# Writing out an inner loop of TensorE in the forward transform of a Fourier tower

## The chip, the cores and the metric

One core of one Trainium2 chip runs the whole program. The metric is device time in microseconds (us) from launch to end, the median of several executions of the same program. All arithmetic is float32.

## The reference, cut to what matters

The input is 64 images of 64x64 pixels with 3 channels. A tower of four Fourier layers works on 64 channels. Each layer adds a spectral convolution (a 2-D Fourier transform, a product with complex 64x64 matrices for 32x16 low modes, and the inverse) to a 64x64 pointwise map, normalizes over batch and pixels, and applies GELU. Attention and two mixtures of experts follow; the change does not touch them.

```python
for l in range(LAYERS):                                   # 4
    sc = _spectral_conv(h, w1r[l] + 1j * w1i[l], w2r[l] + 1j * w2i[l])
    pw = jnp.einsum('bihw,oi->bohw', h, pw_w[l]) + pw_b[l][None, :, None, None]
    y = sc + pw
    ...
    h = jax.nn.gelu(y, approximate=False)
```

## The kernel before, in words

Two images make a pair (128 partitions = 2 x 64 channels), four pairs (Q = 4) make a group, and there are NG = 8 groups, so 32 pairs. Each layer runs in phases, with a meeting of all engines between them (`phase_end`): **forward** (the transform of the layer's input to its low modes), **mix** (the complex product) and **inverse** (back to pixels, pointwise map, statistics). The first layer's forward phase has its own code. Layers 1 to 3 share one body: every engine has an outer hardware loop `Fori(1, L)` over them, so the forward phase that concerns us runs three times, from the same instructions.

In the forward phase every pair goes through five steps:

- SyncE loads the pair's 2 MB from `y_dram` into one of four buffers `hf` (L767 to L792). A buffer is free again when VectorE has turned the pair that was in it.
- ScalarE applies normalization and GELU in four pieces (`scalar_forward`, L843).
- VectorE transposes those four pieces (`px_turn`, L848).
- TensorE does the transform along the width (`w_dft`, L796, matmuls at L803), VectorE transposes the result out of PSUM in two pieces (`w_turn`, L853), and TensorE does the transform along the height (`h_dft`, L809, matmuls at L820).
- VectorE transposes that out of PSUM in two pieces (`h_turn`, L862), and once a group is complete SyncE stores it to `spec_in`.

TensorE's order is written by hand: `w_dft(n)`, then `h_dft(n-1)`, pair after pair. Before `w_dft(n)` it waits for the four transposed pieces of pair n and for the width result of the pair before to be out of PSUM (L797, L798); before `h_dft` it waits for `w_turn` and for the height result of the pair before to be out (L811, L812). VectorE's order, also fixed, is three `px_turn` of pair p, two `w_turn` of pair p-1, the `h_turn` of pair p-2, and the fourth `px_turn` of pair p (L865 to L875). The buffers `t1` and `hT` alternate by the parity of the pair and the PSUM banks are the same for all pairs. The other engines' streams of the forward phase are already written out over all 32 pairs; only TensorE has a hardware loop inside the phase: it does group 0 by itself and then `Fori(1, NG)` over groups 1 to 7, with the four pairs of a group written out in its body. Semaphore thresholds in it are computed from the loop's register and from the layer's.

[...]

Of the kernel before, what the change touches and what calls it, by code (L numbers as in the profile page):

```python
# [102 lines left out]
def build(nc, d, B, out):  # L103

    NP, NG = B // 2, B // GI
# [3 lines left out]
    with ExitStack() as ctx:  # L109
# [684 lines left out]
        def tensor_forward(pe, lf):  # L794
            def w_dft(n, q):

                pe.wait_ge(px_turned, n * 4 + (4 * Q + 4))  # L797
                pe.wait_ge(wdft_turned, n * 2 + 2)  # L798
                pe.sem_inc(waited[pe.engine], 1)
                for s in range(2):  # L800
                    for g in range(4):
                        for c in range(4):
                            mm = pe.matmul(bank[g][QUAD[c], :], fwq[QUAD[g], s * 32:(s + 1) * 32],  # L803
                                           hT[q % 2][QUAD[g], s, :, c * CQ:(c + 1) * CQ],
                                           start=(s == 0), stop=(s == 1), tile_position=(32 * g, 32 * c))
                        if s == 1:
                            mm.then_inc(wdft_done, 1)

            def h_dft(n, q):  # L809

                pe.wait_ge(wdft_turned, n * 2 + 4)  # L811
                pe.wait_ge(hdft_turned, n * 2 + 2)  # L812
                pe.sem_inc(waited[pe.engine], 1)
                for k in range(4):
                    hh, ri = k // 2, k % 2
                    for j in range(4):
                        ro, v = j // 2, j % 2
                        col = (k * 2 + ro) * K1
                        for c in range(4):
                            mm = pe.matmul(bank[4 + c][QUAD[j], 0:256], ghq[QUAD[c], col:col + K1],  # L820
                                           t1[q % 2][QUAD[c], v:4:2, hh, :, ri * M2:(ri + 1) * M2],
                                           start=(k == 0), stop=(k == 3), tile_position=(32 * c, 32 * j))
                mm.then_inc(hdft_done, 1)

            def group(F, first):
                for q in range(Q):
                    n = F * Q + q
                    w_dft(n, q)
                    if q > 0 or not first:
                        h_dft(n - 1, (q - 1) % Q)  # L830

            group(lf * NG, True)
            with pe.Fori(1, NG) as g:
                group(lf * NG + g, False)
            h_dft(lf * NP + (NP - 1), Q - 1)

        def scalar_forward(act, lf):
# [1124 lines left out]
        @block.tensor  # L1962
        def _(pe):
            tensor_spectrum0(pe)
            phase_end(pe, 1)
            tensor_mix(pe, 0, True)
            phase_end(pe, 2)
            tensor_inverse(pe, 0, True)
            phase_end(pe, 3)
            with pe.Fori(1, L) as l:  # L1970
                tensor_forward(pe, l - 1)
                phase_end(pe, l * 3 + 1)
                tensor_mix(pe, l, False)
                phase_end(pe, l * 3 + 2)
                tensor_inverse(pe, l, False)
                phase_end(pe, l * 3 + 3)
            tensor_head(pe)
            phase_end(pe, TOWER + 1)
            tail_tensor(pe)
# [112 lines left out]
```

## Time and profile before

| | before |
|---|---|
| median of 3 runs | 4440.83 us (4436.05 to 4450.31) |
| the profiled execution | 4442.78 us, span 4441.0 us |
| granted TensorE clock, mean | 0.868 |
| busy: PE, PEld, DVE, ACT | 74%, 47%, 54%, 47% |
| mean DMA rate | 252 GB/s |

The span is from the first to the last instruction; the execution's own time is 1.8 us longer. PE is TensorE's matrix multiply, PEld its weight load, which runs beside it; DVE is VectorE, ACT ScalarE, SP SyncE. [...]

### The profile page before, as it was taken

The page shows a single profiled execution, that of the slowest core. Times are in us where ns is not written, and L with a number is a line of the kernel's source. Part 1 is how long each engine was busy: PE and PEld are TensorE (multiplying, and loading weights), DVE is VectorE, ACT ScalarE, POOL GpSimd, SP SyncE. Part 2 cuts the span into 40 slices and gives each one's busy share as a digit, 9 for nine tenths or more (in the row PEclk, how much of TensorE's full clock was granted, in tenths as well). Part 3 has the DMA queues.
Part 4 walks back from the last instruction along what each step waited for, and adds up shares of the span by engine and source line. Part 5 has one row for each costly group of instructions (what it writes and reads, how often), then busy time and mean ns, then how long its engine had stood idle before and what let it go on. Part 6 is the DMA issues. An engine that isn't in the chain of part 4 may idle for free. (4 is left out here: it accounts for less than half of the span.)

```text
span 4441.0 us, 122046 instructions
## 1 busy us (share of the span) xinstructions
PE 3288.5 (74%) x54724; PEld 2081.7 (47%) x54724; DVE 2394.9 (54%) x3232; ACT 2086.9 (47%) x1724; POOL 28.9 (1%) x48
## 2 busy tenths in 40 slices
PE   6878866666888565596886556768877998559777
PEld 4756644455555343473554334745542222543432
DVE  3466668753666587544665777346651000554556
ACT  2133354421666644214665543236667998222321
POOL 0000000000000000000000000000000000100000
PEclk8989988888999888898998778989998999669688
DMA  8978887678999867598999676889996542003053
GB/s 305 351 192 241 238 265 271 256 288 336 345 391 380 295 249 264 228 327 330 381 377 333 248 264 249 321 294 399 391 340 231 190 173 99 10 10 68 1 97 67
DMA packets 181646, 1120.67 MB, mean 252 GB/s; under 512 B 25497, under 2 KB 31841, under 8 KB 107262
## 3 DMA queue, kind: packets, MB, share of 16 engines
q1 hardware_dynamic: 140924, 843.27, 52.7%
q10 hardware_dynamic: 39234, 269.45, 17.5%
q8 instruction: 379, 6.21, 0.5%
q0 software_dynamic: 1024, 1.05, 0.1%
q14 instruction: 85, 0.70, 0.0%
HBM read 708.56 MB, written 405.14 MB: 251 GB/s over the span
## 5 line engine op out<-in xcount | busy, mean ns | idle before, releaser
L602 PEld LDWEIGHTS bank<-fb,arena 64*64 64x64 f32 x16384 | 671.9, 199 | 512.9 <-issue 498.8
L602 PE MATMUL bank<-fb,arena 64*64 64x128 f32 x16384 | 677.9, 293 | 236.8 <-ACT arena L659 183.2
L659 ACT ACTIVATE arena<-bank,pwb 128x1024 f32<-128x1024 f32 x512 | 558.7, 1111 | 472.5 <-PE bank L593 337.0
L703 DVE BATCH_NORM_STATS2 stats<-arena 128x6 f32<-128x512 f32 x1024 | 627.8, 676 | 176.4 <-ACT arena L659 175.9
L843 ACT ACTIVATE arena<-arena,shift,scale 128x1024 f32<-128x1024 f32 x384 | 443.5, 1229 | 438.4 <-DMA arena<-y_dram 437.9
L593 PE MATMUL bank<-arena,wst 64*64 64x512 f32 x4096 | 629.9, 633 | 11.0 <-issue 10.9
L695 DVE STREAM_TRANSPOSE arena<-bank 128x512 f32<-128x512 f32 x512 | 321.1, 685 | 501.5 <-PE bank L579 501.5
L803 PE MATMUL bank<-arena,fwq 32*32 32x512 f32 x6144 | 322.6, 824 | 362.4 <-DVE arena L848 319.3
L651 ACT ACTIVATE arena<-arena,shift,scale 128x2048 f32<-128x2048 f32 x192 | 401.4, 2092 | 353.4 <-issue 206.2
L444 PE MATMUL bank<-arena 64*64 64x128 f32 x8192 | 455.4, 393 | 108.0 <-ACT arena L459 89.0
L444 PEld LDWEIGHTS bank<-arena 64*64 64x64 f32 x8192 | 395.0, 153 | 168.1 <-issue 118.8
L848 DVE STREAM_TRANSPOSE arena<-arena 128x1024 f32<-128x1024 f32 x384 | 440.1, 1203 | 16.2 <-ACT arena L843 16.2
L820 PE MATMUL bank<-arena,ghq 32*32 32x256 f32 x12288 | 366.0, 429 | 49.6 <-issue 45.1
L579 PE MATMUL bank<-arena,ga 64*64 64x512 f32 x2048 | 307.7, 619 | 127.8 <-DMA arena<-spec_out 108.5
L820 PEld LDWEIGHTS bank<-arena,ghq 32*32 32x32 f32 x12288 | 281.7, 111 | 140.5 <-issue 109.1
L803 PEld LDWEIGHTS bank<-arena,fwq 32*32 32x32 f32 x6144 | 101.0, 117 | 496.6 <-issue 486.0
L459 ACT ACTIVATE arena<-arena 64x4096 f32<-64x4096 f32 x32 | 115.9, 3621 | 448.2 <-DMA arena<-spec_in 448.2
L480 DVE STREAM_TRANSPOSE arena<-bank 128x512 f32<-128x512 f32 x256 | 159.5, 683 | 253.3 <-PE bank L444 134.8
L919 PE MATMUL bank<-arena,fc 64*128 64x512 f32 x1024 | 265.3, 626 | 17.9 <-ACT arena L947 16.5
L954 ACT ACTIVATE arena<-bank,fc1b 128x1024 f32<-128x1024 f32 x256 | 267.8, 1122 | 14.3 <-PE bank L919 14.3
L853 DVE STREAM_TRANSPOSE arena<-bank 128x1024 f32<-128x1024 f32 x192 | 227.2, 1221 | 84.9 <-PE bank L803 84.4
L579 PEld LDWEIGHTS bank<-arena,ga 64*64 64x64 f32 x2048 | 115.4, 138 | 249.9 <-issue 236.5
(195 smaller groups left out, 2364.4 us busy)
## 6 DMA issues: line engine op xcount, KB each, us to landing
arena<-y_dram SPq DMA_DIRECT2D x224, 2048.0 KB, 10.2
y_dram<-arena ACTq DMA_DIRECT2D x256, 1024.0 KB, 13.2
arena<-in_w_modes SPq DMA_DIRECT2D x32, 2048.0 KB, 17.2
arena<-spec_in SPq DMA_DIRECT2D x32, 2048.0 KB, 14.7
spec_out<-arena SPq DMA_DIRECT2D x128, 512.0 KB, 15.6
arena<-spec_out SPq DMA_DIRECT2D x112, 512.0 KB, 16.9
spec_in<-arena SPq DMA_DIRECT2D x24, 2048.0 KB, 13.6
spec_in<-arena SPq DMA_DIRECT2D x4, 4096.0 KB, 12.0
```

The lines of the kernel that those rows point to most:

```text
L444: mm = pe.matmul(bank[4 * v + q][ROW[half], k * 2 * B:(k + 1) * 2 * B], w_sb[u][ROW[row], mode, :], s_sb[u][ROW[row], :, :, mode], start=( ...
L579: mm = pe.matmul(bank[2 * v + r][CHAN[par], :], ga[k_p, r * S:(r + 1) * S], grp[p // Q % 2][k_p, :, par * Q + q, :], start=True, stop=True ...
L593: mm = pe.matmul(bank[4 + T % 2 * 2 + i][CHAN[v], :], wst[CHAN[i], :], hin[p % 3][CHAN[i], px:px + BK], start=False, stop=True, tile_posit ...
L602: mm = pe.matmul(hpx(bank[4 + T % 2 * 2 + i][CHAN[v], :])[:, :, j * S:(j + 1) * S], a2[p % 2][CHAN[i], v, :, 4 * T + j], hpx(fb2[CHAN[i], :]),
L651: act.activation(x, x, ACT.Gelu, bias=shift[:], scale=scale[:]).then_inc(h_ready, 1)
L659: act.activation(hpx(yout[u])[:, :, T * BK:(T + 1) * BK], banks[:, 4 + T % 2 * 2:6 + T % 2 * 2, :], ACT.Identity, bias=pwb[:]).then_inc(y_ ...
L695: dve.transpose(a2[p % 2][:, :, v * HB + c0:v * HB + c0 + 16, :].rearrange("p v c r -> p c v r"), banks[:, 2 * v:2 * v + 2, :].rearrange(" ...
L703: dve.bn_stats(stats[:, p * 48 + 6 * t:p * 48 + 6 * t + 6], hpx(yout[p % 2])[:, i, T * BK:(T + 1) * BK]).then_inc(y_seen, 1)
L803: mm = pe.matmul(bank[g][QUAD[c], :], fwq[QUAD[g], s * 32:(s + 1) * 32], hT[q % 2][QUAD[g], s, :, c * CQ:(c + 1) * CQ], start=(s == 0), st ...
L820: mm = pe.matmul(bank[4 + c][QUAD[j], 0:256], ghq[QUAD[c], col:col + K1], t1[q % 2][QUAD[c], v:4:2, hh, :, ri * M2:(ri + 1) * M2], start=( ...
L843: act.activation(x, x, ACT.Gelu, bias=shift[:], scale=scale[:]).then_inc(f_ready, 1)
L848: dve.transpose(hT[p % 2][:, :, 16 * v:16 * v + 16, :].rearrange("p s h c -> p h s c"), hf[p % Q][:, v * 2 * BK:(v + 1) * 2 * BK].rearrang ...
```

## The change

TensorE's groups of the forward phase are all written out. Group 0 still begins without the `h_dft` of a pair before it. Nothing that TensorE computes and no order changes, the semaphore thresholds are the same numbers (they still hold the layer's register), and no other engine's stream is touched. The outer loop over layers stays.

```diff
-            group(lf * NG, True)
-            with pe.Fori(1, NG) as g:
-                group(lf * NG + g, False)
+            for g in range(NG):
+                group(lf * NG + g, g == 0)
             h_dft(lf * NP + (NP - 1), Q - 1)
```

## Rows read from the trace of the kernel before

**Rows 1.** Busy time by stage: the three forward phases, one mix, one inverse
```profile
core 0: us, PE busy (x) PEld busy (x) DVE busy (x) ACT busy (x) POOL busy (x), PEclk, DMA share, GB/s
619.00:942.80 323.80, 198.60 (x6144) 128.48 (x6144) 259.59 (x256) 149.07 (x129) 0.00 (x0) 0.83 0.71 267
942.80:1096.80 154.00, 112.97 (x2048) 97.23 (x2048) 58.11 (x72) 28.97 (x8) 0.00 (x0) 0.85 0.87 327
1096.80:1517.20 420.40, 329.58 (x5636) 219.63 (x5636) 245.91 (x400) 267.91 (x194) 0.00 (x0) 0.89 0.94 357
1517.20:1861.50 344.30, 203.79 (x6144) 127.27 (x6144) 260.48 (x256) 149.19 (x129) 0.00 (x0) 0.81 0.67 252
...
2444.20:2788.60 344.40, 206.51 (x6144) 126.84 (x6144) 260.48 (x256) 149.08 (x129) 0.00 (x0) 0.80 0.68 251
```

**Rows 2.** Busy time by stretch: groups 1, 2, 3, 4, 6 of phase one
```profile
663.60:709.50 45.90, 27.81 (x768) 16.54 (x768) 32.70 (x33) 21.70 (x20) 0.00 (x0) 0.77 0.64 231
709.50:744.90 35.40, 23.92 (x768) 16.46 (x768) 32.19 (x33) 15.12 (x14) 0.00 (x0) 0.86 0.78 289
744.90:783.50 38.60, 22.80 (x768) 15.84 (x768) 35.67 (x35) 19.03 (x17) 0.00 (x0) 0.87 0.84 307
783.50:828.90 45.40, 27.99 (x768) 16.55 (x768) 29.25 (x30) 20.18 (x18) 0.00 (x0) 0.80 0.57 210
864.30:898.60 34.30, 22.79 (x768) 16.03 (x768) 32.14 (x33) 18.55 (x16) 0.00 (x0) 0.90 0.82 308
```

**Rows 3.** The same view: groups 2 to 7 of each phase, and group 1 of phases two and three
```profile
709.50:929.90 220.40, 144.06 (x4608) 97.20 (x4608) 188.10 (x186) 93.95 (x82) 0.00 (x0) 0.86 0.74 277
1566.90:1611.00 44.10, 26.46 (x768) 15.18 (x768) 32.65 (x33) 20.40 (x19) 0.00 (x0) 0.80 0.66 240
1611.00:1847.10 236.10, 149.53 (x4605) 96.26 (x4608) 189.10 (x186) 94.43 (x82) 0.00 (x0) 0.84 0.70 259
2492.40:2536.90 44.50, 27.56 (x768) 15.52 (x768) 32.75 (x33) 21.36 (x19) 0.00 (x0) 0.79 0.65 238
2536.90:2775.60 238.70, 151.60 (x4608) 95.73 (x4608) 188.88 (x186) 94.24 (x82) 0.00 (x0) 0.82 0.69 256
```

**Rows 4.** Instruction queue in 663.6:709.5, then 709.5:929.9 and 1611.0:1847.1: packets, MB, share
```profile
q8 instruction: 6, 0.10, 0.8%
...
q8 instruction: 9, 0.15, 0.3%
...
q8 instruction: 18, 0.29, 0.5%
```

**Rows 5.** Weight loads in order of time, group 1 of phase one: start, us, what, idle before
```profile
663.80 0.56 PEld L803 LDWEIGHTS bank<-arena,fwq 32*32 32x32 f32 x33 [3.18 <-issue]
...
671.15 1.24 PEld L820 LDWEIGHTS bank<-arena,ghq 32*32 32x32 f32 x58 [2.49 <-issue]
675.96 0.32 PEld L803 LDWEIGHTS bank<-arena,fwq 32*32 32x32 f32 x32 [3.58 <-issue]
...
686.05 0.56 PEld L803 LDWEIGHTS bank<-arena,fwq 32*32 32x32 f32 x33 [3.18 <-issue]
...
693.03 1.00 PEld L820 LDWEIGHTS bank<-arena,ghq 32*32 32x32 f32 x63 [3.55 <-issue]
697.21 0.32 PEld L803 LDWEIGHTS bank<-arena,fwq 32*32 32x32 f32 x32 [3.18 <-issue]
...
706.37 0.13 PEld L820 LDWEIGHTS bank<-arena,ghq 32*32 32x32 f32 x2 [2.56 <-issue]
709.68 0.54 PEld L803 LDWEIGHTS bank<-arena,fwq 32*32 32x32 f32 x32 [3.18 <-issue]
```

**Rows 6.** The same view, at the turn from group 3 to group 4
```profile
773.18 2.74 PEld L820 LDWEIGHTS bank<-arena,ghq 32*32 32x32 f32 x127 [0.15 <-issue]
783.72 0.22 PEld L803 LDWEIGHTS bank<-arena,fwq 32*32 32x32 f32 x7 [7.80 <-issue]
788.47 0.28 PEld L803 LDWEIGHTS bank<-arena,fwq 32*32 32x32 f32 x32 [4.53 <-issue]
```

**Rows 7.** Waits, 663.6:709.5 (one row), then 864.3:898.6: us in total, times, longest
```profile
DVE arena L862 <- PE bank L820: 10.9, 4, 3.5
...
PE bank L803 <- DVE arena L848: 11.5, 4, 3.0
DVE arena L862 <- PE bank L820: 2.2, 2, 1.1
```

## The prediction

> **What bounds the kernel now.** I read the busy time by stage first. The three forward phases take 323.8, 344.3 and 344.4 us, 1012.5 of the span's 4441.0 [rows 1]. They run the same instructions on the same amount of data, and yet the first is 20 us shorter. VectorE has the most work in them, about 260 us each, so 64 to 84 us per phase are idle even on the busiest engine.
>
> Then I cut the phase at TensorE's groups. A group of four pairs takes 35.4 or 34.3 us in some passes of the loop (groups 2 and 6), and 45.9 or 45.4 us in others (groups 1 and 4), with the same 768 matmuls [rows 2]. In the short ones VectorE is busy 32.1 of 34.3 us: it is the bound, at 8.6 us a pair, and TensorE waits for its fourth transpose before each `w_dft`, 11.5 us in four waits [rows 7]. In the long ones VectorE waits for TensorE instead: 10.9 us before `h_turn` where the short group has 2.2 [rows 7].
>
> What sets the two kinds apart is in the instruction queue [rows 4]. During group 1, whose code is reached for the first time, six 16 KB packets of instructions arrive on q8. During all of groups 2 to 7 only nine arrive in phase one, and eighteen in phase two. So most passes of the loop run on instructions that are already at the engine, and some do not. The weight loads show how the packets cost time [rows 5]: in group 1 the stream of `h_dft` loads, otherwise dense, breaks for 2.49, 3.55 and 2.56 us in the middle (at 671.15, 693.03 and 706.37), with nothing that it waits for. In the short groups there is no such break. The other cost shows at the turn into group 4 [rows 6]: the loop's first instructions have to be brought back, TensorE is idle 7.80 us where an ordinary turn costs 3.18 (at 709.68 [rows 5]), and 4.53 us more seven loads later.
>
> **The change part by part.**
> *Removed: the loop's branch.* Where the code is present, the turn shows the same 3.18 us of idle time as the steps inside a group [rows 5], all of it waiting for VectorE. The branch is hidden, and removing it is worth nothing. *Removed: the turns that miss.* A turn with a miss costs 7.80 + 4.53 - 3.18 = 9.2 us at the weight loads. Phase one has one of them, with nine packets; phase two has eighteen packets [rows 4], so two misses, and phase three, as long as phase two [rows 3], I take to have two as well: five in all. One more miss, 9.2 us, and the breaks of the packets that follow it make up the 16 to 18 us by which groups 2 to 7 of those phases are longer [rows 3]. *Added: every group is now reached for the first time.* Each takes its six packets in the way that group 1 does. I take the sum over whole groups, not over stalls, so that removed misses and added stalls are counted once.
>
> Groups 2 to 7 now take 220.4 + 236.1 + 238.7 = 695.2 us [rows 3]. A group of straight code takes 45.9, 44.1 and 44.5 us, mean 44.83 [rows 2, 3]. Groups 2 to 7 written out take five of these and a sixth that ends with its last load, without the 3.18 us of waiting: 6 x 44.83 - 3.2 = 265.8, three phases 797.4. The difference is +102 us. Group 0, group 1 and the last `h_dft` are straight code already and stay.
>
> A correction goes with where the breaks fall. From the break at 671.15 to that at 693.03 the rows have 379 weight loads (192 a pair), three packets, so a packet holds about 126 loads with their matmuls, and a group of 768 loads is six packets and ten or so loads. A packet's edge that falls in `w_dft` or right at the start of `h_dft` shows no break, because the fetch then runs during TensorE's wait for VectorE; one inside `h_dft` shows. In group 1, three of four pairs have a visible one; those pairs last 12.16, 11.16 and 12.47 us, the fourth 10.09 (differences of the `w_dft` starts [rows 5]). Moving the edges ten to twelve loads earlier with each group, I count 21 or 22 of the 24 later pairs with an edge inside `h_dft`. At 11.93 and 10.09 us, scaled by 44.83/45.9 for the three phases, that is 21.5 x 11.65 + 2.5 x 9.85 - 3.2 = 271.9 a phase, 815.7, and +120 us. Between +102 and +120 I take +110, since the position count rests on four pairs.
>
> *The other phases.* All of TensorE's code behind the forward phase moves in memory by some 600 KB, so its packet edges fall elsewhere. The mix and the inverse are straight code now too, and in the inverse the DMA engines are busy 94% [rows 1]. I take zero; a few us a phase either way, 10 us in all, go into the range. SyncE and ScalarE keep their order: their loads wait for VectorE's `px_turn`, and come later by as much as VectorE does. DMA share in the long groups is lower (0.64 against 0.82 [rows 2]), so there is room for 63 more packets of 16 KB in three phases.
>
> The sum is 4442.8 + 110 = 4553 for the profiled execution, which lies 2 us above the median of the three runs; so 4551.
>
> [...]
>
> **The rivals.**
> *A. Straight code streams ahead once no branch interrupts it (faster).* The mechanism would be that the stalls of group 1 are an after-effect of a jump, and that a long straight run gets its packets in time. Then only the misses go: every pair lasts as in the short groups, 6 x 34.85 - 3.2 = 205.9 us a phase, 617.7 in all, -77 us, 4366. For it speaks the miss [rows 6]. Against it: group 1 of phase one comes after over 600 us of TensorE code without a taken branch (layer 0 is straight code), and it is the slowest of the three, 45.9. Chance 0.08. [...]
> *B. The stalls mostly miss the chain (about the same, or slower by little).* The edges would fall where TensorE waits. The point of balance is (695.2/3 + 3.2)/24 = 9.8 us a pair; below it the change wins. The pair at 675.96 lasts 10.09, close to that, but three of four do not. Within 0.3% (13 us) needs 9.6 to 10.0 us a pair. Chance 0.04; and 0.06 for 10.0 to 10.5 a pair, +15 to +50 us.
> *C. The fetches cost more with the new edges (much slower).* Two edges in a pair, one in `w_dft` and one late in `h_dft`, give 12.47 us [rows 5]. If every pair lasted so, 24 x 12.47 - 3.2 = 296.1 a phase, +193 us, 4634. Half the pairs so and half at 11.65 give +156, 4597. Chance of more than 4600: 0.07.
> *D. Nothing changes in what the engine is fed*: excluded, since a program without the inner branch has no way to run group 2 from group 1's instructions.
>
> **How the numbers follow.** The forecast, 4495 to 4600, has 0.75: from +52 (later pairs at 10.5 us on average: the 10.09 above for three in four, an edge that shows for one) to +157 (12.0 us on average, between the 11.65 and the 12.47 above). A's 0.08 lies at 4366, too far to take in. About 0.3% (13 us) is what a measurement of this kernel can tell from no change. Slower by more than that: 0.75 + 0.06 + 0.07 = 0.88; the same 0.04; faster 0.08. Range 4492 to 4602.
>
> **What would show it.** In the changed profile: the three forward phases have nearly equal lengths, about 370 us each (now 323.8, 344.3, 344.4), with about 49 packets on q8 in each; each group about 45 us with VectorE at 29 to 33 us of it; breaks of 2 to 4 us inside `h_dft` in most pairs; no idle stretch of 7.8 us before a `w_dft`; the mix and the inverse at 154 and 420 us. I am wrong if later groups fall to 35 us while six packets arrive in each (rival A), or if group length differs strongly by group with the same number of packets (then where edges fall decides, rivals B and C).

## The result: slower by 1.7 to 2.0%, all of it in the three forward phases

The written-out kernel takes 4514.5 us in the median of four runs against 4438.4 us before, ratio 1.0175 with a 95% interval of 1.0113 to 1.0237. One of the four runs (4601.8 us) had a clock of 0.76 against 0.86 in the others and is left out of the ratio. Timed again in a later session (run e11 below) it took 4512.1 against 4421.9 us, ratio 1.0202 (1.0164 to 1.0240). The profiled execution took 4513.87 us, 71.1 us more than the one of before.

The same stages as in [rows 1], in the changed kernel (stretch, its length, busy us of each engine, clock, DMA share, GB/s):

```profile
622.30:982.70 360.40, 220.95 (x6144) 125.24 (x6144) 261.81 (x256) 149.21 (x129) 0.00 (x0) 0.79 0.65 241
982.70:1136.50 153.80, 113.70 (x2048) 96.13 (x2048) 58.27 (x72) 28.97 (x8) 0.00 (x0) 0.87 0.87 328
1136.50:1556.00 419.50, 325.34 (x5636) 217.21 (x5636) 245.74 (x400) 268.44 (x194) 0.00 (x0) 0.90 0.95 358
1556.00:1917.80 361.80, 217.20 (x6144) 121.97 (x6144) 261.93 (x256) 149.20 (x129) 0.00 (x0) 0.80 0.65 240
2498.60:2860.40 361.80, 220.53 (x6144) 124.38 (x6144) 262.02 (x256) 149.19 (x129) 0.00 (x0) 0.79 0.65 240
```

The forward phases have become equal, 360.4, 361.8 and 361.8 us, 1084.0 in all where there were 1012.5. That is +71.5 us, the whole difference of the two executions. A mix and an inverse together, from the end of one forward phase to the start of the next, take 573.3 and 580.8 us where they took 574.4 and 582.7. The unit of comparison from here on is the group or the pair; groups (0 to 7) and pairs (0 to 31) of a phase are numbered from 0. Cut at the groups, as in [rows 2, 3]: groups 1 to 5 of phase one, then groups 2 to 7 of each phase.

```profile
668.50:713.20 44.70, 25.10 (x768) 14.94 (x768) 32.57 (x33) 21.01 (x19) 0.00 (x0) 0.83 0.65 237
713.20:758.50 45.30, 27.12 (x768) 15.34 (x768) 32.61 (x33) 17.17 (x16) 0.00 (x0) 0.84 0.65 234
758.50:802.00 43.50, 29.18 (x768) 16.28 (x768) 32.82 (x33) 18.10 (x17) 0.00 (x0) 0.77 0.67 243
802.00:845.70 43.70, 27.84 (x768) 15.15 (x768) 32.71 (x33) 19.35 (x17) 0.00 (x0) 0.77 0.67 242
845.70:889.50 43.80, 28.71 (x768) 14.77 (x768) 32.78 (x33) 18.92 (x18) 0.00 (x0) 0.81 0.66 242
713.20:970.40 257.20, 167.02 (x4608) 93.11 (x4608) 190.81 (x187) 94.25 (x82) 0.00 (x0) 0.80 0.65 239
1647.50:1905.60 258.10, 164.78 (x4608) 91.69 (x4608) 190.93 (x187) 95.15 (x83) 0.00 (x0) 0.81 0.64 238
2592.00:2848.20 256.20, 165.29 (x4608) 92.03 (x4608) 190.92 (x187) 95.03 (x83) 0.00 (x0) 0.81 0.65 240
```

Every group shown lasts 43.5 to 45.3 us; the 34.3 and 35.4 us of [rows 2] are gone, and so are the long turns. Groups 2 to 7 take 257.2 + 258.1 + 256.2 = 771.5 us where they took 695.2 [rows 3]. VectorE's busy time in them has hardly moved (190.8 us against 188.1 in phase one), so it waits. The instruction queue in groups 2 to 7 of phase one, which carried nine packets [rows 4]:

```profile
q8 instruction: 37, 0.61, 0.9%
```

In the whole execution q8 has 443 packets of 16 KB where it had 379, while q14, the other queue of kind instruction, has 85 in both. TensorE's stream is the only one that differs, so q8 brings TensorE's instructions.

The weight loads of group 2, of which only the loads after a long idle stretch are shown (start, us, what, count, idle before). The trace has 64 loads and 64 matmuls for a `w_dft` and 128 and 128 for an `h_dft`, twice the matmuls of the source: 6144 and 12288 of each in the 96 pairs.

```profile
713.32 0.32 PEld L803 LDWEIGHTS bank<-arena,fwq 32*32 32x32 f32 x32 [3.17 <-issue]
...
720.18 1.21 PEld L820 LDWEIGHTS bank<-arena,ghq 32*32 32x32 f32 x68 [1.44 <-issue]
724.56 0.27 PEld L803 LDWEIGHTS bank<-arena,fwq 32*32 32x32 f32 x32 [3.18 <-issue]
...
732.50 0.15 PEld L820 LDWEIGHTS bank<-arena,ghq 32*32 32x32 f32 x7 [2.09 <-issue]
735.94 0.32 PEld L803 LDWEIGHTS bank<-arena,fwq 32*32 32x32 f32 x32 [3.29 <-issue]
...
743.25 1.45 PEld L820 LDWEIGHTS bank<-arena,ghq 32*32 32x32 f32 x73 [2.61 <-issue]
747.88 0.27 PEld L803 LDWEIGHTS bank<-arena,fwq 32*32 32x32 f32 x32 [3.18 <-issue]
...
755.28 0.17 PEld L820 LDWEIGHTS bank<-arena,ghq 32*32 32x32 f32 x12 [3.07 <-issue]
758.67 0.32 PEld L803 LDWEIGHTS bank<-arena,fwq 32*32 32x32 f32 x32 [3.22 <-issue]
```

Each of the four `h_dft` breaks once, for 1.44, 2.09, 2.61 and 3.07 us, with nothing that the engine waits for. The word `issue` on a row of loads does not say that by itself, it only names no releaser: the 3.17 us before 713.32 end with it too, while the matmuls from 713.35 on wait 2.72 us for VectorE's `px_turn`. In the breaks the rows of the matmuls name no releaser either (0.86, 1.61, 2.12 and 2.58 us), the program has no wait between the first and the last matmul of an `h_dft`, and each time a packet on q8 ends 1.5 us before the loads go on. In the kernel before, groups 2 and 6 of phase one, which ran on kept instructions, had no such break: no idle stretch inside their `h_dft` is over 0.63 us. Where the breaks fall also gives the size of a packet: counted in TensorE's instructions, every break in the middle of a DFT of phase one lies a multiple of 256 behind the one before it, give or take one instruction (the last three above 511, 257 and 511).

### The profile page after: what moved, and what is told of

Its sections match the earlier page's. It is cut to its first block and busy times, and to the rows that moved or that the text cites. A ratio compares the mean times of both kernels' runs of the same rounds, so it can differ in the third digit from the quotient of the medians.

```text
span 4512.1 us, 122001 instructions
## 1 busy us (share of the span) xinstructions
PE 3332.8 (74%) x54724; PEld 2057.2 (46%) x54724; DVE 2400.6 (53%) x3232; ACT 2088.0 (46%) x1724; POOL 28.9 (1%) x48
## 5 line engine op out<-in xcount | busy, mean ns | idle before, releaser
L803 PE MATMUL bank<-arena,fwq 32*32 32x512 f32 x6144 | 350.0, 916 | 328.3 <-DVE arena L847 326.3
L444 PEld LDWEIGHTS bank<-arena 64*64 64x64 f32 x8192 | 385.0, 154 | 173.1 <-issue 112.9
L820 PE MATMUL bank<-arena,ghq 32*32 32x256 f32 x12288 | 378.2, 430 | 109.4 <-issue 104.7
L820 PEld LDWEIGHTS bank<-arena,ghq 32*32 32x32 f32 x12288 | 267.9, 111 | 244.7 <-issue 210.9
```

Of the source, the lines that this page charges most:

```text
L444: mm = pe.matmul(bank[4 * v + q][ROW[half], k * 2 * B:(k + 1) * 2 * B], w_sb[u][ROW[row], mode, :], s_sb[u][ROW[row], :, :, mode], start=( ...
```

## The experiments

Two theories stand against each other at first. **Fetch:** what a pair costs is set by whether its instructions must be brought in; a loop saves time only as long as its body is kept. **Loop turns:** what matters is the loop's turn itself, or the length of the code in some other way.

### e1: a loop over two pairs

```diff
-            group(lf * NG, True)
-            with pe.Fori(1, NG) as g:
-                group(lf * NG + g, False)
+            def two(n, first):
+                for q in range(2):
+                    w_dft(n + q, q)
+                    if q > 0 or not first:
+                        h_dft(n + q - 1, (q - 1) % 2)
+            two(lf * NP, True)
+            with pe.Fori(1, NP // 2) as g:
+                two(lf * NP + g * 2, False)
```

> TensorE's loop of the forward phase has two pairs in its body (15 passes, some 780 instructions, three packets of 16 KB) instead of four. Fetch theory (the time of a pair is set by whether its instructions must be brought in): after the first pass or two no packet arrives in the loop, no turn misses, and pairs last 8.6 us as in the short groups of the kernel before. A phase is then about 7 + 18 + 30 x 8.6 + 13 = 296 us or a little more, 300 x 3 = 900 against 1012.9, so about 4330 us in all, ratio 0.975. Rival, that turns of the loop cost time by themselves: 15 turns a phase in place of 7, at the 9.2 us that a missed turn costs, would give phases of 400 us or more and a kernel slower than the written-out one.

Measured: 4319.9 us, ratio 0.9742 (0.9708 to 0.9776). The three forward phases, and the instruction queue in the first:

```profile
620.00:917.70 297.70, 189.64 (x6144) 128.11 (x6144) 259.44 (x256) 149.24 (x129) 0.00 (x0) 0.86 0.77 289
1491.50:1791.60 300.10, 189.06 (x6144) 128.70 (x6144) 259.44 (x256) 149.24 (x129) 0.00 (x0) 0.86 0.76 287
2366.90:2665.20 298.30, 186.91 (x6144) 122.98 (x6144) 259.08 (x256) 149.23 (x129) 0.00 (x0) 0.87 0.77 289
```
```profile
q8 instruction: 6, 0.10, 0.1%
```

Against the written-out kernel that is six packets instead of 49 in phase one, fifteen passes of a loop instead of none, and 896.1 us instead of 1084.0 for the same arithmetic in the same order. The turns are not what costs. This version beats both kernels, the changed one by some 190 us.

### e2: a loop over eight pairs

```diff
             group(lf * NG, True)
-            with pe.Fori(1, NG) as g:
-                group(lf * NG + g, False)
+            group(lf * NG + 1, False)
+            with pe.Fori(1, NG // 2) as g:
+                group(lf * NG + g * 2, False)
+                group(lf * NG + g * 2 + 1, False)
```

> Groups 0 and 1 written out, then a loop of three passes over two groups each (about 3120 instructions, over twelve packets). Fetch theory: the body is larger than what stays at the engine, so all 18 later groups of the three phases take their packets, as in the written-out kernel, and the two taken turns of each phase miss: 9.2 us each less what is hidden. 4514 + 6 x 7 = about 4555 us, 49 to 53 packets a phase, groups of about 44 us. Rival, that written-out code is slow for another reason than its length and that a loop gives the time back: near the kernel before, 4440.

Measured: 4540.6 us, ratio 1.0240 (1.0194 to 1.0286).

```profile
620.30:983.70 363.40, 219.66 (x6144) 126.39 (x6144) 261.81 (x256) 149.19 (x129) 0.00 (x0) 0.79 0.64 239
1562.70:1925.90 363.20, 220.70 (x6144) 126.32 (x6144) 261.80 (x256) 149.09 (x129) 0.00 (x0) 0.78 0.64 239
2504.50:2871.20 366.70, 221.41 (x6144) 126.12 (x6144) 261.81 (x256) 149.08 (x129) 0.00 (x0) 0.79 0.64 237
```
```profile
q8 instruction: 51, 0.84, 0.9%
```

A loop whose body is longer than what is kept behaves as written-out code does: 1093.3 us in the phases, 9 more than written out. The two turns of a phase were not what I had expected, though. TensorE is idle for 3.7 to 4.3 us before the `w_dft` behind them, 0.6 to 1.1 more than the 3.18 of an ordinary step, and not the 7.0 to 8.3 us of the missed turns of the kernel before; why these are cheap was not looked into. I had expected some 40 us for the whole kernel and it was 26 between the medians. The profiled executions differ by 19, 9 of it in the forward phases and 10 in other stages, which I did not take apart. A loop by itself gives nothing back. With e1 this settles the first question for fetch.

### e3 and e4: the same code, moved

Ahead of the first group of each forward phase, 64 waits that are already satisfied, once in the written-out kernel (e3) and once in the kernel before (e4):

```diff
+            for i in range(64):
+                pe.wait_ge(phase_done, ENGINES * 3)
```

> The written-out kernel with 64 instructions (waits that are already satisfied) put ahead of the first group in each forward phase, where TensorE idles anyway: every packet edge falls 32 weight loads earlier. Fetch theory: the length of each phase stays within 6 us (360 to 362), but the pattern of pairs moves: in the written-out kernel the fast pairs of 9.1 to 9.5 us are numbers 24, 26 and 30 of a phase, where one edge falls within the first 70 or so loads; here they are about ten pairs earlier, 14, 16, 18 and 20, and number 3 and 5 (9.1 to 9.8 us) turn slow. Rival, that the differences between pairs come from DMA traffic or the group's store and not from packet edges: the fast pairs stay at 24, 26 and 30.

> The kernel before with the same 64 instructions ahead of the first group. Fetch theory: hits and misses of the loop's turns depend on where its body of just over six packets lies between packet edges, so the number of packets in a phase (21, 32 and 32 before) and its length (324, 344, 344) change together, at 10 to 12 packets and about 20 us for one more missed turn. If the misses were a matter of chance in time rather than of place, the counts would stay between 21 and 32.

Two such waits in a row turned out to become one instruction: the profile of e3 counts 99 instructions more than that of the written-out kernel, so 33 a phase, half of what I had reckoned with. e3 took 4543.5 us in its one run, 1099.8 in the forward phases (368.3, 365.3, 366.2). That is 3.5 to 7.9 us more a phase than written out, where I had expected at most 6. The pattern moved. Pairs 1 and 3 of phase one, 10.4 and 9.1 us long in the written-out kernel, last 11.9 and 11.3. The fast ones, numbers 24 and 26 there (9.2 and 9.1 us), are 20, 22 and 24 here (9.3, 9.1 and 9.3), about half of the ten pairs that I had expected for twice the shift. These are differences of the `w_dft` starts. The breaks themselves show the shift more exactly: the one in pair 4 comes after 134 weight loads in the written-out kernel and after 118 here, and 16 loads with their matmuls are 32 instructions. Of e3, pairs 20 to 23:

```profile
859.35 0.32 PEld L803 LDWEIGHTS bank<-arena,fwq 32*32 32x32 f32 x32 [3.18 <-issue]
...
868.61 0.19 PEld L803 LDWEIGHTS bank<-arena,fwq 32*32 32x32 f32 x10 [3.18 <-issue]
...
879.54 0.27 PEld L803 LDWEIGHTS bank<-arena,fwq 32*32 32x32 f32 x32 [3.18 <-issue]
...
888.64 0.17 PEld L803 LDWEIGHTS bank<-arena,fwq 32*32 32x32 f32 x5 [3.18 <-issue]
...
899.08 0.27 PEld L803 LDWEIGHTS bank<-arena,fwq 32*32 32x32 f32 x32 [3.17 <-issue]
```

So the place of a packet's edge in the pair decides whether it shows.

e4 brought more than was forecast: 4385.0 us in its one run, **faster** than the kernel before, whose eleven runs in the same session lie between 4420.8 and 4469.0 (median 4436.4), although only instructions that do nothing were added. Its forward phases, and the queue in the second:

```profile
629.20:938.50 309.30, 191.31 (x6144) 122.39 (x6144) 259.80 (x256) 149.23 (x129) 0.00 (x0) 0.85 0.74 279
1520.20:1832.40 312.20, 190.84 (x6144) 121.30 (x6144) 259.44 (x256) 149.23 (x129) 0.00 (x0) 0.85 0.74 276
2411.00:2723.70 312.70, 191.90 (x6144) 122.62 (x6144) 259.68 (x256) 149.21 (x129) 0.00 (x0) 0.84 0.74 276
```
```profile
q8 instruction: 15, 0.25, 0.3%
```

No turn misses any more; all five missed turns of the kernel before are gone.

### e7 to e10: where the loop's body lies

A theory for that: a packet holds 256 instructions, the body is 1559 instructions (its loads, matmuls and other TensorE instructions from one turn to the next in the trace), six packets and 23 more, and TensorE keeps fewer than eight. In the kernel before the body begins (worked out from the breaks) some 20 instructions ahead of an edge, so it touches eight packets, the eighth with its last few instructions. The same holds for any start 1 to 22 instructions ahead of an edge; everywhere else the body touches seven. e7 and e8 are e4 with 24 and 256 waits. e9 and e10 put 510 and 64 waits elsewhere, once, ahead of the first layer's mix, so that nothing stands in the forward phase:

```diff
             phase_end(pe, 1)
+            for i in range(510):
+                pe.wait_ge(phase_done, ENGINES)
             tensor_mix(pe, 0, True)
```

> The kernel before with only 24 satisfied waits ahead of the first group in each forward phase. Place theory: the loop's body is 1559 instructions, which is six packets of 256 and 23 more; in the kernel before it begins some 20 instructions ahead of a packet's edge, so it touches eight packets, the last one with its last few instructions and the branch, and eight is one too many to keep. 24 instructions later it touches seven. So no turn misses, 13 to 15 packets a phase, phases of 308 to 313 us as with 64 waits, about 4380 us, ratio 0.985 to 0.99. If the gain of the 64 waits came from delaying TensorE by a few us instead, 24 of them would leave misses, 21 to 32 packets a phase and 4400 to 4440 us.

> The same with 256 waits, a whole packet: the body lies between edges exactly as in the kernel before. Place theory: missed turns come back, 22 to 34 packets a phase, groups of 45 us among groups of 34.3, and the phases are 324 to 350 us and up to 8 more, since 256 waits take longer than TensorE idles there. Delay theory: none, as with 64.

> The kernel before with 510 satisfied waits once, ahead of the first layer's mix, where TensorE idles some 20 us. Two waits in a row become one instruction (the padded kernels have 13, 33 and 129 instructions more a phase for 24, 64 and 256 waits), so these are 256 instructions, one packet: everything behind lies between packet edges as in the kernel before, and the forward phases hold no padding. Place theory, with the body's start some 20 instructions ahead of an edge (0 and 13 more: eight packets touched, missed turns; 33 and 129 more: seven, none): missed turns are back, one to three a phase, 21 to 41 packets. Rival, that any padding of 33 instructions or more does away with them: 13 to 15 packets, no missed turn.

> The same place, 64 waits, so 33 instructions, and none of them in the forward phase. Place theory: seven packets touched, no missed turn, 14 to 16 packets a phase, phases of 305 to 310 us, about 4370 us, ratio 0.983 to 0.990. Rival, that the waits had to stand ahead of the phase's first group: 21 to 32 packets and 4400 to 4450 us.

e7 and e8 came out the other way round than I had written. The count of instructions in their profiles told why (two waits are one instruction), and e9 and e10 were built on that. All placements, sorted by how far the body is moved:

```
kernel   instructions   packets in the    forward phases, us     time of the kernel, us (median of
         added ahead    three phases                             the kernel before in that session)
before   0              21, 32, 32        323.8 344.3 344.4      4442.8 (profiled)
e7       13 a phase     30, 32, 32        348.4 351.0 347.7      4482.3 (4423.4), ratio 1.0168 (1.0118 to 1.0217)
e10      32 once        13, 15, 15        308.0 314.5 314.1      4373.2 (4421.9), ratio 0.9896 (0.9858 to 0.9935)
e4       33 a phase     13, 15, 15        309.3 312.2 312.7      4385.0 (4436.4), one run
e8       129 a phase    13, 15, 15        307.9 317.9 315.5      4368.4 (4423.4), one run
e9       255 once       21, 32, 23        322.1 344.5 331.2      4450.9 (4421.9), one run
```

Counted from the first instruction of the loop's body to the break that shows the edge, the body starts 18 instructions ahead of an edge in the kernel before, 5 ahead in e7, 14 or 15 behind one in e10 and e4, 111 behind in e8, and again 18 or 19 ahead in e9. Missed turns occur in the first, second and last (five, six and four of them), where eight packets are touched, and in none of the other three. Of e9, the queue in phases one, two and three:

```profile
q8 instruction: 21, 0.34, 0.4%
...
q8 instruction: 32, 0.52, 0.6%
...
q8 instruction: 23, 0.38, 0.5%
```

and one of its missed turns, which looks like [rows 6]:

```profile
882.93 0.23 PEld L803 LDWEIGHTS bank<-arena,fwq 32*32 32x32 f32 x8 [7.67 <-issue]
887.41 0.28 PEld L803 LDWEIGHTS bank<-arena,fwq 32*32 32x32 f32 x31 [4.25 <-issue]
```

Neither the delay of a few us nor the presence of padding explains that; e10 has no padding in the phase and e9 has the most before it. Even with eight packets touched only some turns miss, and not the same ones in each phase. There is a pattern in the four profiles with missed turns (the kernel before, e6, e7, e9; six turns a phase): of the 28 turns that follow a group whose packets had just been fetched none missed, and of the 44 that follow a group run on kept instructions 18 did. What decides among those 44 stays open.

e7 was slower than the kernel before by 1.7%, or by 1.3% if the medians of all its six and all eleven runs beside it are compared, for 13 instructions that do nothing. Its six missed turns against five account for part of it. Another part lies in the groups that are fetched: in e7 the second pair behind a missed turn has a break too, after 189 loads, and pair 17 of phase one lasts 10.5 us where it lasted 8.0.

### e5 and e6: the same two kernels with most of the data traffic taken away

Both kernels leave out seven eighths of every load from `y_dram` in the forward phases, so their results are not those of the reference; VectorE, ScalarE and TensorE do the same work on what lies in the buffers.

```diff
-                sp.dma_start(hf[q], y_dram[g * Q + q]).then_inc(f_loaded[q], 16)
+                sp.dma_start(hf[q][:, 0:BK], y_dram[g * Q + q][:, 0:BK]).then_inc(f_loaded[q], 16)
```

> The written-out kernel with the forward phase's loads from y_dram cut to an eighth (512 of 4096 columns a buffer); the rest of the buffer keeps old numbers, so that part of the input is left out. Theory a, that a packet of instructions is slow to come because the DMA engines are full of data (share 0.66 in a written-out group): with them almost idle the breaks inside h_dft shrink under 1 us and groups fall to about 36 us. Theory b, that the time of a fetch is its own, whatever the traffic: groups stay at 42 to 44 us and the breaks at 2 us or more.

> The kernel before with the same cut of the loads. Beside the written-out one it gives the difference without data traffic. Theory a: the forward phases of the two differ by less than 30 us in all. Theory b: by 50 to 75 us, as with the traffic (71.2), with groups of 34.3 us where no packet comes and the same five missed turns.

Measured, one run each: 4350.2 us written out (e5), 4348.9 with the loop (e6). The written-out kernel's forward phases, then its groups 2 and 3, and the packets in group 3:

```profile
623.60:926.80 303.20, 191.00 (x6144) 121.66 (x6144) 259.70 (x256) 148.97 (x129) 0.00 (x0) 0.86 0.30 105
1503.50:1811.80 308.30, 193.50 (x6144) 123.69 (x6144) 260.02 (x256) 148.97 (x129) 0.00 (x0) 0.85 0.30 103
2390.40:2695.70 305.30, 192.10 (x6144) 123.18 (x6144) 259.77 (x256) 148.98 (x129) 0.00 (x0) 0.85 0.30 104
701.20:738.50 37.30, 25.12 (x768) 15.25 (x768) 32.55 (x34) 18.54 (x16) 0.00 (x0) 0.86 0.26 87
738.50:772.70 34.20, 22.66 (x768) 15.36 (x768) 32.24 (x33) 18.55 (x16) 0.00 (x0) 0.90 0.29 95
```
```profile
q8 instruction: 6, 0.10, 1.0%
```

The packets still come, six a group and 49 in phase one, and now most of them cost next to nothing: group 3 lasts 34.2 us with VectorE busy 32.2 of it, as in the short groups [rows 2]. In the weight loads of that group the longest idle stretch inside an `h_dft` is 0.58 us. The phases sum to 916.8 us written out and 913.6 with the loop (302.2, 316.7, 294.7), against a difference of 71.5 with the traffic.

One place in e5 keeps its long break, pair 29 of each phase, with 4.24, 2.58 and 2.57 us; no other break in the middle of a DFT of its phases is over 1.2 (I had expected all of them under 1). It is also the place where the traffic was not cut: SyncE loads the weights of the next mix there, 2 MB at a time, and the 16 DMA engines are full (the stretch around the first of these breaks; the last two numbers are the DMA share, 1.03, and the GB/s):

```profile
888.00:894.00 6.00, 2.24 (x113) 1.64 (x100) 3.68 (x4) 0.00 (x0) 0.00 (x0) 1.00 1.03 349
```

Theory a holds: whether a fetch is late depends on the data traffic (DMA share 0.65 in groups 2 to 7 of the written-out kernel's phase one, 0.29 in group 3 here). What grows is not the packet's own transfer, which by the shares of q8 is about 1 us in both cases (six packets at 1.0% of 16 engines in 34.2 us, 37 at 0.9% in 257.2). So it is the time until it is served; that it waits behind data on those engines is the likely reading, and the profile does not show it.

Fetching is still not quite free. The third phase of e6, with 14 packets and no missed turn, took 294.7 us, the written-out phases of e5 303.2 to 308.3. With the traffic the same comparison is 312.7 us (e4, 15 packets) against 361.8. And e6 still has three missed turns, which now cost 4.5 to 5.0 us each at the weight loads, where the one of [rows 6] cost 9.2.

### e11: the written-out kernel again

> The written-out kernel unchanged, timed again beside the kernel before. 49 to 51 packets a phase as in its first profile, about 4514 us, and a narrower spread than that of the kernel before, since it has no turn that can hit or miss: ratio 1.012 to 1.024.

Measured: 4512.1 us, ratio 1.0202 (1.0164 to 1.0240), six runs within 4503.7 to 4522.1, where the eleven of the kernel before lay within 4397.4 and 4456.3. The spread shrank by two thirds, as expected from code without a turn that can miss. That the missed turns make the spread is not shown: e7 has six of them in its profile, and its six runs lie within 4464.5 and 4486.2.

## Why the prediction was right, and where its sum was off

**Direction, place and mechanism** were right. The time went where forecast, into groups 2 to 7 of the forward phases; the phases became equal; the packets in them rose to 49, 51 and 51; a mix and an inverse together stayed within 2 us.

**The branch at nothing:** right. e1 has fifteen passes a phase and pairs of 8.6 us on average (pairs 8 to 23).

**Missed turns and straight groups:** five missed turns went, every group now has its breaks. The base of the sum, 6 x 44.83 - 3.2 a phase or +102 us, was read from group 1 alone. Measured are +76.3 us in groups 2 to 7 (771.5 - 695.2); the rest of the forward phases became 4.8 us shorter, which gives the 71.5. Group 1's three breaks were 2.49, 3.55 and 2.56 us, while those of group 2 begin at 1.44. The last groups are shorter too: in phase one pairs 24, 26 and 30 last 9.2, 9.1 and 9.4 us, with an edge, by the count of 256, within the first 20 loads of `h_dft` and no break at it; that the fetch then runs in TensorE's wait, as the prediction had it, fits the trace (a packet is on q8 from 886.68 to 888.00 us, in the 3.18 us without a load before pair 24 starts at 889.64) and e3, where the fast pairs moved with the edges, from 24 and 26 to 20, 22 and 24. It is not so at every edge ahead of an `h_dft`: eleven loads into the `w_dft` of pair 27, at 920.92, the loads break for 1.28 us.

**The correction for the place of the edges** is the term that was mis-sized most, by its sign. Its count was nearly right: an edge shows in 19 of the 24 later pairs (all of groups 2 to 5, though some breaks there are under 1 us, and pairs 25, 27 and 29), where I had 21 or 22. Its price was not: I took 11.65 us for a pair with a visible edge, from three pairs, and pairs 8 to 23 of the three phases last 11.0 to 11.1 on average. With 11.05 for 20 pairs and 9.3 for four, less 3.2, the sum would have been 255.0 a phase, 765 in all, +70 us, close to the measured +76.3. So the forecast of +110 came to +71 for the profiled pair. It stayed in the range because the range was wide: its lower end stood for 10.5 us a pair, and 10.85 were measured in phase one (257.2 + 3.2, over 24). The five missed turns that it took away were those of one execution; e9, with the body in the same place, had four.

The prediction also saw room for 63 more packets in a DMA share of 0.64. Their bytes fit, but at a mean share of 0.65 they came late all the same.

**Rival A** (straight code streams ahead) is refuted at this traffic, with breaks of 1.44 to 3.07 us a pair in group 2 at a DMA share of 0.65. In e5, where the share is 0.30, it comes close to true: 0.58 us at most inside an `h_dft` of group 3, and no more than 1.2 in any break outside pair 29. **Rival B** fell with 10.85 us a pair, where it needed 10.5 or less. **Rival C** needed 12.47 us a pair; only single pairs reach that.

What the prediction did not see is how much was to be had in the other direction. It priced the loop's hits and misses as they stood, and took the five misses as given. They came from where the body lay: e10 moves it and gains 1.0%. A body of half the length (e1) gains 2.6%, which takes in the same missed turns and, beyond them, the packets of group 1.

## What to carry to other kernels

Before writing out a loop, count its packets in the instruction queue: passes that bring none pay no fetch, and writing them out costs a fetch for every packet, which showed here as idle time with no cause where the engine issues without waiting and the DMA engines are busy with data (1.44 to 3.07 us a break in group 2, share 0.65). A loop body paid here if it was kept whole, edges included (seven packets touched, or a body of half the length), so try the shortest that the buffers' parities allow. Here that was two pairs and not four or eight.

## What the runs showed of the hardware that I had not expected

Instructions that do nothing moved the time of the kernel by +1.3 to +1.7% and -1.0% (e7, e10). For e10, which has none of them in the forward phase, only the place of the code is left as the reason.

TensorE kept and reused a body that touches seven packets (13 to 15 packets a phase and no missed turn in e4, e8 and e10), and missed turns with one that touches eight (five, six and four of them in the kernel before, e7 and e9). The body of e10 touches seven, and in phase one it runs for the passes of groups 3 to 7, each entered by the loop's branch, without a packet on q8 from 753 to 920 us.

Groups with breaks also ran at a lower granted clock. It averages 0.77 to 0.84 in the written-out groups, and 0.86 to 0.90 in groups of the same code in e5 and in the short groups of [rows 2]. Every record of it in the profiles of the two kernels and of e5 is 0.50 or 1.00. The 64 loads of one `w_dft` of the written-out kernel, whose `h_dft` before had a break of 2.67 us, fell in a stretch at the lower level and took 2.4 us from the first to the last. In e5, with no break in the pair before, the same 64 loads ran at the upper level and took 1.5:

```profile
845.80:848.20 2.40, 2.35 (x48) 1.09 (x64) 2.40 (x3) 2.40 (x3) 0.00 (x0) 0.50 0.68 164
738.70:740.20 1.50, 1.47 (x49) 0.86 (x64) 1.50 (x2) 0.00 (x0) 0.00 (x0) 1.00 0.41 97
```

How much of the 71 us comes by that way was not measured by itself, and neither was that the breaks are what lowers the clock.
